# Image attention: the last 32 keys of four sub-steps gathered, turned by one transpose and weighed by values padded with zeros

## The chip, the cores and the metric

One Trainium2 chip, one core of it. The metric is the device time of one execution in microseconds (us). All times below are of that core.

## What is computed

The reference is a chain of eight gated layers on an image sequence `x` (4 batches, 512 tokens, width 128), each with its own attention or feed-forward part. The change touches the first one alone:

```python
def _layernorm(x, axis=-1, eps=1e-05): ...
def _L0_xattn_ref(image_embeds, latents, ln1_g, ln1_b, ln2_g, ln2_b, Wq, Wkv, Wo):
    x = layer_norm(image_embeds, ln1_g, ln1_b)      # context: 4 x 154 x 128
    l = layer_norm(latents, ln2_g, ln2_b)           # latents: 4 x 512 x 128
    q = l @ Wq
    kv_in = jnp.concatenate([x, l], axis=1)         # 666 keys
    k, v = jnp.split(kv_in @ Wkv, 2, axis=-1)
    # 16 heads of 64; softmax(q k / 8) v; heads joined; @ Wo
x = x + jnp.tanh(g_xattn[0]) * _L0_xattn_ref(ctx_1024, _layernorm(x, axis=-1), ...)
```

Every one of the 512 queries of a batch attends to 666 keys, the 512 latents and the 154 context rows, in 16 heads of width 64. 666 keys are five tiles of 128 and a rest of 26.

## The kernel before

All eight layers run one after the other as one program. Each engine has its own instruction stream, written out by hand; streams meet only in semaphores, and every engine does its instructions in the order of its stream.

**The unit of work in the first layer.** Two heads are projected together, a *group* (32 of them: 4 batches of 8 pairs). A group has two *units* of 256 queries (64 units), and a unit four *sub-steps*, (h, j) = (0,0), (0,1), (1,0), (1,1): one head h and one tile of 128 queries j each (256 sub-steps). The streams all loop over `image_steps()`, and the loop index i is the sub-step whose scores are made. In iteration i:

- TensorE (`image_pe`, L593) makes the scores of sub-step i (`image_scores_pe`, L683: four bf16 matmuls, into one of two slots of two PSUM banks). If i % 4 is 0 it weighs tiles 0 to 2 of the unit two back, if it is 2 tiles 3 to 5 (`image_weigh_pe`, L709), and then turns the two spread tiles (L615). Then it turns the probabilities of sub-step i-2 (`image_turn_pe`, L694): six fp32 transposes, four into bank 4, two into bank 5 (the last of 26 rows). In even iterations comes one of the four parts of the next group's projection (`image_project_pe`, L475, into bank 7).
- VectorE (`image_ve`, L715) multiplies the finished unit by its inverse sums (L740, if i % 4 is 3), takes the largest score of sub-step i from PSUM (L744), in odd iterations makes the low bf16 halves of the projection part (`image_lows_ve`, L798 to L813), takes the reciprocal of the sums (L752, if i % 4 is 0), and copies bank 5 of sub-step i-2 to SBUF (L758, the event `kept_b`). For sub-step (0,0) it also makes the low half of these two tiles itself (L763, `low_c`).
- ScalarE (`image_ac`, L816) makes the exponentials of sub-step i (L837; it waits for the maximum), keeps the spread tiles (L846, if i % 4 is 2; once per unit), copies bank 4 of sub-step i-2 to SBUF (L852, `kept_a`), and keeps the high halves of the projection part (`image_keep_ac`, L881 to L895).
- GpSimd (`image_po`, L897) spreads the inverses (L934), splits the finished unit (L942), and makes the low halves of the turned probabilities of sub-step i-3: tiles 0 to 3 (L963, 512 wide, `low_a`) and, except for (0,0), tiles 4 and 5 (L963, 256 wide, `low_b`). In the first 160 iterations or so it also splits the next layer's weights, one piece every fourth iteration (L979, L980, L983).

**Products are three bf16 matmuls** (high by low, low by high, high by high), so a tile of probabilities is weighed by 3 matmuls a head: 64 columns of values as the weights, 256 queries as the moving side. The two heads of the pair write the two halves of the partitions of bank 6. A unit has 6 x 3 x 2 = 36 of them.

**Banks.** Banks 4 and 5 are single: the transposes of a sub-step wait for `kept_a` and `kept_b` of the sub-step before (`low_c` in place of `kept_b` after (0,0)). Bank 7 is single too: a projection part waits until VectorE has made the lows of the part before.

Beside the regular iterations there are chores once per batch: the layer norms of the next batch on VectorE (L405 to L421) and its transposes, and the output projection of the batch before (eight pairs by three matmuls for each of four tiles, L475), which shares bank 7.

Of the kernel before, what the change touches and what calls it, by code (L numbers as in the profile page):

```python
# [9 lines left out]
ALU = mybir.AluOpType  # L10
# [126 lines left out]
def constants():  # L137
# [33 lines left out]
    for part in range(3):  # L171
# [18 lines left out]
        "clear": "filled", "tokens": "filled", "wo_low": "filled", "mixed_low": "low_b", "summed": "router_steps", "ranked": "routed",  # L190
        "places": "placed", "clean": "router_steps", "padded": "router_steps", "relative": "router_steps", "delta": "router_steps",
# [33 lines left out]
class Kernel:  # L225
# [293 lines left out]
    def image_memory(self):  # L519
# [3 lines left out]
        self.v = [self.place(KT0, 2, P, dt=BF16) for _ in range(3)]  # L523
# [3 lines left out]
        self.probs_t = [self.place(2, KT0, 2 * P) for _ in range(2)]  # L527
        self.sums = [self.place(4) for _ in range(4)]
        self.inverse = [self.place(4) for _ in range(2)]
# [3 lines left out]
        self.probs_parts = [t.rearrange("p h t n -> p (h t n)").bitcast(BF16).rearrange("p (h t n s) -> p h t n s", h=2, t=KT0, s=2)  # L533
# [59 lines left out]
    def image_pe(self, pe):  # L593
        w = self.w[0]
        pe.wait_ge(*self.at("dma_const", 16))
        pe.wait_ge(*self.at("clean", 1))
# [9 lines left out]
        for i in self.image_steps():  # L606
# [3 lines left out]
            if back is not None:  # L610
                self.image_weigh_pe(pe, back, ((0, 1, 2), None, (3, 4, 5))[part])
# [29 lines left out]
    def image_project_pe(self, pe, n, part):  # L641
# [12 lines left out]
        elif part == 2:  # L654
            self.bank(pe, 7, "v_low", 3 * n + 2)
# [7 lines left out]
            m = self.products(pe, side[:, 3 * P:4 * P], lambda s: c[:, s, c0 + P:c0 + 2 * P], lambda s: values[s], True, True)  # L663
        else:
            self.bank(pe, 7, "v_low", 3 * n + 3)
# [20 lines left out]
    def image_turn_pe(self, pe, i):  # L686
        prob = self.probs[i % 3]
        pe.wait_ge(*self.at("exp", i + 1))
        for bank, tiles, name in ((4, range(0, 4), "kept_a"), (5, range(4, KT0), "kept_b")):
            ps = self.bank(pe, bank, *((name, i) if bank == 4 or (i % 4) else ("low_c", i // 4)))  # L690
            for t in tiles:
                rows = min(P, KEYS0 - t * P)
                c = (t - tiles[0]) * P
                m = pe.transpose(ps[0:rows, c:c + P], prob[:, t * P:t * P + rows], self.eye)  # L694
            m.then_inc(self.mark("turned_a" if bank == 4 else "turned_b"))

    def image_weigh_pe(self, pe, u, tiles):
        n = u // 2
        if tiles[0] == 0:
            pe.wait_ge(*self.at("low_a", 4 * u + 3))  # L700
            pe.wait_ge(*self.at("v_low", 3 * n + 3))
            self.bank(pe, 6, "mixed", u + 1)
        else:
            pe.wait_ge(*self.at("low_b", 4 * u + 3))
            pe.wait_ge(*self.at("low_c", u))
        for t in tiles:
            for which, (of_values, of_probs) in enumerate(((0, 1), (1, 1), (0, 0))):
                for h in (0, 1):
                    m = pe.matmul(self.out_bank[64 * h:64 * h + 64, 0:2 * P], self.v[n % 3][:, t, of_values, 64 * h:64 * h + 64],  # L709
                                  self.probs_parts[u % 2][:, h, t, :, of_probs], start=t == 0 and which == 0,  # L710
                                  stop=t == KT0 - 1 and which == 2)
        if tiles[-1] == KT0 - 1:
            m.then_inc(self.mark("weighed"))

    def image_ve(self, ve):  # L715
        x, xn = self.x, self.xn
        ve.memset(self.bank_b, 0.0).then_inc(self.mark("clean"))
        for v in self.v:
            ve.memset(v[:, KT0 - 1, :, :], 0.0)
# [15 lines left out]
        for i in self.image_steps():  # L735
# [12 lines left out]
            if back is not None and part == 0:  # L748
# [3 lines left out]
                ve.reciprocal(self.inverse[back % 2], self.sums[back % 4]).then_inc(self.mark("inverted"))  # L752
            if 2 <= i < SUBS + 2:
                u, _, _, _, h, j = self.image_sub(i - 2)
                if u >= 2:
                    ve.wait_ge(*self.at("weighed", u - 1))
                ve.wait_ge(*self.at("turned_b", i - 1))
                ve.tensor_copy(self.probs_t[u % 2][:, h, 4:KT0, j * P:(j + 1) * P],  # L758
                               self.bank_b[:, 0:2 * P].rearrange("p (t n) -> p t n", t=2)).then_inc(self.mark("kept_b", i - 2))
                if (h, j) == (0, 0):  # L760
# [136 lines left out]
    def image_po(self, po):  # L897
# [68 lines left out]
        for _ in pieces:  # L966
            pass
# [1832 lines left out]
```

## Time and profile before

| what | value |
|---|---|
| median of 3 runs | 1933.74 us (1933.63 to 1936.42) |
| profiled execution, its own time | 1927.72 us |
| its span, first to last instruction | 1925.9 us |
| mean granted TensorE clock | 0.875 |
| busy share of the span: TensorE, VectorE, ScalarE, GpSimd | 78%, 61%, 42%, 39% |
| the first layer's attention in the span | about 35 to 712 us |
| busiest groups | GpSimd L963 372.6 us, TensorE L694 218.0, VectorE L744 216.3, ScalarE L837 209.2 |

In the profile a duration is that of one instruction from start to end. Instructions of one engine overlap at their ends, so what an instruction costs in a busy stream is the distance from its start to the next start, which is shorter. "PEld" is TensorE's weight load. An idle time in brackets stands before the instruction, with what ended it; "issue" is time in which the engine waited for nothing that the profile shows.

### The profile page before, as it was taken

To read this page: it belongs to the slowest core of one execution; us is meant where nothing else is said; L and a number is where in the kernel's file an instruction comes from. 1 tells how busy PE (TensorE), PEld (TensorE's weight loads), DVE (VectorE), ACT (ScalarE), POOL (GpSimd) and SP (SyncE) were. 2 spreads that over 40 slices of the span, in tenths; PEclk is the share of its full clock that TensorE was granted. 3 is DMA by queue.
4 is the path that set the end of the run, shared out by engine and by line. 5 is a ranking of instruction groups with operands and counts; after the bars stand their busy time and mean duration, and the time that the engine had idled before them with its cause. 6 is when DMAs were issued, how large, how long until landed. Compare 5 with 4: busy or idle time off the path is not lost.

```text
span 1925.9 us, 31970 instructions
## 1 busy us (share of the span) xinstructions
PE 1497.9 (78%) x11459; PEld 982.9 (51%) x11581; DVE 1175.3 (61%) x2856; ACT 802.1 (42%) x1803; POOL 754.6 (39%) x906
## 2 busy tenths in 40 slices
PE   4899979979998977574278789958976885568877
PEld 2677757766776765452255345524443333324444
DVE  4777677767767655538847657644565555644443
ACT  3677657747765644320034245533212542201111
POOL 3688678857756863500012343000002101233330
PEclk9999999999999997776568799989986987778887
DMA  6233211211211112400000000000000000000000
GB/s 241 63 102 106 74 55 42 55 36 38 54 41 45 52 33 72 161 5 1 0 1 1 11 4 1 1 1 1 1 1 1 1 1 1 1 0 6 1 6 11
DMA packets 35442, 63.93 MB, mean 33 GB/s; under 512 B 7527, under 2 KB 25026, under 8 KB 34131
## 3 DMA queue, kind: packets, MB, share of 16 engines
q1 hardware_dynamic: 33815, 59.77, 10.4%
q0 software_dynamic: 1472, 2.12, 0.4%
q8 instruction: 95, 1.56, 0.3%
q14 instruction: 60, 0.49, 0.1%
HBM read 30.59 MB, written 12.66 MB: 22 GB/s over the span
## 4 chain that ended last, share of the span: by engine, by line
PE 63%; DVE 23%; issue 4%; POOL 4%; ACT 4%; DMA 1%; SPq 0%; DVEq 0%; ACTq 0%; POOLq 0%
PE banks L475 15%; PE banks L694 8%; PE banks L709 6%; PE banks L683 6%; PE banks L1876 3%; DVE xn L421 3%; PE banks L1859 2%; PE banks L450 2%; DVE work L744 2%; PE banks L2546 2%; DVE norm_room L405 1%; PE banks L2497 1%; PE banks L1785 1%; PE banks L1826 1%; POOL work L963 1%
## 5 line engine op out<-in xcount | busy, mean ns | idle before, releaser
L963 POOL TENSOR_TENSOR work<-work 128x512 bf16<-128x512 f32 (+1 forms) x448 | 372.6, 861 | 48.3 <-ACT work L852 45.0
L837 ACT ACTIVATE work<-banks,work 128x666 f32<-128x666 f32 x256 | 209.2, 817 | 200.6 <-DVE work L744 165.7
L415 POOL TENSOR_TENSOR norm_room<-norm_room,minus_half 128x4 f32<-128x4 f32 x48 | 50.1, 1044 | 542.3 <-DVE norm_room L410 542.3
L744 DVE TENSOR_REDUCE work<-banks 128x1 f32<-128x666 f32 x256 | 216.3, 845 | 61.2 <-PE banks L683 60.8
L694 PE MATMUL banks<-const,work 128*128 128x128 f32 (+1 forms) x1536 | 218.0, 279 | 31.2 <-ACT work L852 26.1
L694 PEld LDWEIGHTS banks<-const,work 128*128 128x128 f32 (+1 forms) x1536 | 155.9, 135 | 53.0 <-ACT work L837 29.4
L758 DVE COPY work<-banks 128x256 f32<-128x256 f32 x256 | 106.9, 418 | 122.2 <-PE banks L694 122.1
L683 PE MATMUL banks<-work 128*128 128x154 bf16 (+1 forms) x932 | 170.6, 302 | 11.5 <-DMA work<-work 6.4
L475 PE MATMUL banks<-work,weights_b 128*128 128x512 bf16 (+1 forms) x830 | 157.4, 347 | 13.3 <-DVE work L2200 5.6
L709 PE MATMUL banks<-work 128*64 128x256 bf16 x2304 | 158.6, 282 | 8.3 <-POOL work L963 7.1
L852 ACT ACTIVATE work<-banks 128x512 f32<-128x512 f32 x256 | 151.2, 591 | 9.5 <-PE banks L694 9.4
L450 PE MATMUL banks<-const,xn 128*128 128x128 f32 x176 | 40.7, 374 | 141.4 <-DVE xn L421 89.3
L683 PEld LDWEIGHTS banks<-work 128*128 128x128 bf16 x1024 | 98.1, 99 | 88.6 <-DMA work<-work 6.6
L1953 DVE TENSOR_REDUCE work<-banks 128x2 f32<-128x308 f32 x192 | 86.8, 473 | 79.2 <-PE banks L1831 45.1
L709 PEld LDWEIGHTS banks<-work 128*64 128x64 bf16 x2304 | 120.4, 110 | 28.1 <-POOL work L963 10.2
L456 ACT ACTIVATE xt<-banks 128x512 f32<-128x512 f32 x48 | 28.7, 597 | 246.3 <-PE banks L450 246.1
L475 PEld LDWEIGHTS banks<-work,weights_b 128*128 128x128 bf16 (+1 forms) x840 | 83.0, 100 | 83.9 <-issue 18.3
L2688 POOL TENSOR_TENSOR work<-work 128x512 bf16<-128x512 f32 x64 | 66.3, 1043 | 142.8 <-DVE work L2645 142.8
L1932 ACT ACTIVATE work<-banks 128x256 f32<-128x256 f32 (+1 forms) x256 | 87.4, 382 | 59.5 <-PE banks L1863 26.9
L450 PEld LDWEIGHTS banks<-const,xn 128*128 128x128 f32 x176 | 26.7, 187 | 153.6 <-DVE xn L421 72.6
L1859 PE MATMUL banks<-work 128*128 128x256 bf16 (+1 forms) x256 | 66.4, 292 | 14.1 <-ACT work L1924 11.6
L475 PE MATMUL banks<-weights_c 128*128 128x128 bf16 (+2 forms) x288 | 65.9, 260 | 0.0
(390 smaller groups left out, 3006.8 us busy)
## 6 DMA issues: line engine op xcount, KB each, us to landing
work<-work SPq DMA_DIRECT2D x128, 166.5 KB, 3.0
sorted<-in_pads SPq DMA_DIRECT2D x10, 838.5 KB
weights_b<-in_weights SPq DMA_DIRECT2D x1, 4120.0 KB, 23.9
work<-scratch SPq DMA_DIRECT2D x64, 64.0 KB, 2.0
weights_b<-in_weights SPq DMA_DIRECT2D x1, 2824.0 KB, 9.8
weights_a<-in_weights SPq DMA_DIRECT2D x1, 2056.0 KB, 8.5
weights_a<-in_weights SPq DMA_DIRECT2D x1, 2050.0 KB, 10.1
work<-work SPq DMA_DIRECT2D x32, 64.0 KB, 1.9
```

Of the source, the lines that this page charges most:

```text
L450: i = pe.transpose(ps[:, j * P:j * P + rows], src[0:rows, j, :], self.eye[0:rows, 0:rows])
L475: m = pe.matmul(out, left(a), right(b), start=start and n == 0, stop=stop and n == 2)
L683: m = pe.matmul(slot[:, a:z], lhs, k[:, h, part, a:z], start=part == 0, stop=part == 1)
L694: m = pe.transpose(ps[0:rows, c:c + P], prob[:, t * P:t * P + rows], self.eye)
L709: m = pe.matmul(self.out_bank[64 * h:64 * h + 64, 0:2 * P], self.v[n % 3][:, t, of_values, 64 * h:64 * h + 64], self.probs_parts[u % 2][:, ...
L744: ve.tensor_reduce(self.neg_max[i % 4], self.slot[i % 2][:, 0:KEYS0], AX_X, ALU.max, negate=True).then_inc(self.mark("max"))
L758: ve.tensor_copy(self.probs_t[u % 2][:, h, 4:KT0, j * P:(j + 1) * P], self.bank_b[:, 0:2 * P].rearrange("p (t n) -> p t n", t=2)).then_inc ...
L837: ac.activation(self.probs[i % 3], self.slot[i % 2][:, 0:KEYS0], ACT.Exp, bias=self.neg_max[i % 4], accum_out=self.sums[u % 4][:, 2 * j + ...
L852: ac.activation(self.probs_t[u % 2][:, h, 0:4, j * P:(j + 1) * P], self.bank_a.rearrange("p (t n) -> p t n", t=4), ACT.Copy).then_inc(self ...
L963: po.tensor_tensor(parts[:, :, :, 0], exact, parts[:, :, :, 1], ALU.subtract).then_inc(self.mark(event, i - 3))
L1859: m = pe.matmul(bank, left, a.q4[b % 2][:, g, cols], start=True, stop=s != 4)
L1932: ac.activation(out, self.bank_of(k, HALF)[0:rows_n, :], ACT.Exp).then_inc(self.mark("exp4", s, n))
```

## The change

Keys 634 to 665, the last 32 of the 666, are taken out of the tiles. After its exponentials each sub-step has these 32 columns copied by VectorE into a quarter of a 128-wide tile `rest` in SBUF. After the fourth sub-step of a unit this tile is turned by one transpose, kept, and split once. It then holds four quarters of 32 rows, one for each (h, j). The weighing of tile 5 is replaced by six matmuls of 128 columns by 128 queries: for each j a value tile of 128 rows that holds the 32 keys of head 0 in quarter j, columns 0 to 63, those of head 1 in quarter 2 + j, columns 64 to 127, and zeros elsewhere. The full tiles are five, and in the fifth the values of its last 6 keys are zero, since the rest holds them. The four-fold last context rows are made by GpSimd once per batch (`four_times_po`), so that one projection yields the values in all four quarters; these are then kept by ScalarE and subtracted by VectorE in four pieces of 32 x 64 in place of one of 26 x 128.

The sixth transpose of each sub-step falls away, VectorE's copy of bank 5 is 128 wide in place of 256, its `low_c` moves from sub-step (0,0) to (1,1), where it is a 128-wide copy and a 128-wide subtraction, and GpSimd makes tile 4 of all four sub-steps, 128 wide. The clearing of bank 5 at the start, and TensorE's wait for it, are gone.

```diff
@@ -520,17 +520,19 @@
...
-        self.v = [self.place(KT0, 2, P, dt=BF16) for _ in range(3)]
+        self.v = [self.place(KT0 + 1, 2, P, dt=BF16) for _ in range(3)]
...
-        self.probs_t = [self.place(2, KT0, 2 * P) for _ in range(2)]
+        self.probs_t = [self.place(2, KT0 - 1, 2 * P) for _ in range(2)]
+        self.rest, self.rest_t = ([self.place(P) for _ in range(2)] for _ in range(2))
...
+        self.ctx_last = self.place(2, P, dt=BF16)
...
-        self.probs_parts = [t.rearrange("p h t n -> p (h t n)").bitcast(BF16).rearrange("p (h t n s) -> p h t n s", h=2, t=KT0, s=2)
+        self.probs_parts = [t.rearrange("p h t n -> p (h t n)").bitcast(BF16).rearrange("p (h t n s) -> p h t n s", h=2, t=KT0 - 1, s=2)
@@ -608,7 +609,7 @@
...
-                self.image_weigh_pe(pe, back, ((0, 1, 2), None, (3, 4, 5))[part])
+                self.image_weigh_pe(pe, back, ((0, 1, 2), None, (3, 4))[part])
@@ -652,7 +653,7 @@
...
-            self.bank(pe, 7, "v_low", 3 * n + 2)
+            self.bank(pe, 7, "v_low", 6 * n + 5)
@@ -660,9 +661,11 @@
...
-            m = self.products(pe, side[:, 3 * P:4 * P], lambda s: c[:, s, c0 + P:c0 + 2 * P], lambda s: values[s], True, True)
+            if n % PAIRS == 0:
+                pe.wait_ge(*self.at("four_times", b))
+            m = self.products(pe, side[:, 3 * P:4 * P], lambda s: self.ctx_last[:, s, :], lambda s: values[s], True, True)
...
-            self.bank(pe, 7, "v_low", 3 * n + 3)
+            self.bank(pe, 7, "v_low", 6 * n + 6)
@@ -686,37 +689,44 @@
...
-        for bank, tiles, name in ((4, range(0, 4), "kept_a"), (5, range(4, KT0), "kept_b")):
-            ps = self.bank(pe, bank, *((name, i) if bank == 4 or (i % 4) else ("low_c", i // 4)))
-            for t in tiles:
-                rows = min(P, KEYS0 - t * P)
-                c = (t - tiles[0]) * P
-                m = pe.transpose(ps[0:rows, c:c + P], prob[:, t * P:t * P + rows], self.eye)
-            m.then_inc(self.mark("turned_a" if bank == 4 else "turned_b"))
+        ps = self.bank(pe, 4, "kept_a", i)
+        for t in range(4):
+            m = pe.transpose(ps[:, t * P:(t + 1) * P], prob[:, t * P:(t + 1) * P], self.eye)
+        m.then_inc(self.mark("turned_a"))
+        ps = self.bank(pe, 5, *(("kept_b", i) if i % 4 < 3 else ("low_c", i // 4)))
+        m = pe.transpose(ps[:, 0:P], prob[:, 4 * P:5 * P], self.eye)
+        if i % 4 == 3:
+            pe.wait_ge(*self.at("gathered", i))
+            m = pe.transpose(ps[:, P:2 * P], self.rest[i // 4 % 2], self.eye)
+        m.then_inc(self.mark("turned_b"))
...
-            pe.wait_ge(*self.at("v_low", 3 * n + 3))
+            pe.wait_ge(*self.at("v_low", 6 * n + 6))
...
+        orders = ((0, 1), (1, 1), (0, 0))
...
-            for which, (of_values, of_probs) in enumerate(((0, 1), (1, 1), (0, 0))):
+            for which, (of_values, of_probs) in enumerate(orders):
...
-                    m = pe.matmul(self.out_bank[64 * h:64 * h + 64, 0:2 * P], self.v[n % 3][:, t, of_values, 64 * h:64 * h + 64],
-                                  self.probs_parts[u % 2][:, h, t, :, of_probs], start=t == 0 and which == 0,
-                                  stop=t == KT0 - 1 and which == 2)
-        if tiles[-1] == KT0 - 1:
+                    pe.matmul(self.out_bank[64 * h:64 * h + 64, 0:2 * P], self.v[n % 3][:, t, of_values, 64 * h:64 * h + 64],
+                              self.probs_parts[u % 2][:, h, t, :, of_probs], start=t == 0 and which == 0, stop=False, skip_group_check=True)
+        if tiles[-1] == KT0 - 2:
+            rest = self.halves(self.rest_t[u % 2])
+            for of_values, of_probs in orders:
+                for j in (0, 1):
+                    m = pe.matmul(self.out_bank[:, j * P:(j + 1) * P], self.v[n % 3][:, KT0 - 1 + j, of_values, :], rest[:, :, of_probs],
+                                  start=False, stop=(of_values, of_probs) == orders[-1], skip_group_check=True)
...
-        ve.memset(self.bank_b, 0.0).then_inc(self.mark("clean"))
...
-            ve.memset(v[:, KT0 - 1, :, :], 0.0)
+            ve.memset(v[:, KT0 - 2:, :, :], 0.0)
@@ -750,17 +760,22 @@
...
+            if 1 <= i < SUBS + 1:
+                u, s = (i - 1) // 4, (i - 1) % 4
+                if s == 0 and u >= 2:
+                    ve.wait_ge(*self.at("turned_b", 4 * u - 4))
+                ve.wait_ge(*self.at("exp", i))
+                ve.tensor_copy(self.rest[u % 2][:, 32 * s:32 * (s + 1)], self.probs[(i - 1) % 3][:, KEYS0 - 32:]).then_inc(self.mark("gathered", i - 1))
...
-                ve.tensor_copy(self.probs_t[u % 2][:, h, 4:KT0, j * P:(j + 1) * P],
-                               self.bank_b[:, 0:2 * P].rearrange("p (t n) -> p t n", t=2)).then_inc(self.mark("kept_b", i - 2))
-                if (h, j) == (0, 0):
-                    ve.wait_ge(*self.at("kept_b", i - 2))
-                    parts = self.probs_parts[u % 2][:, h, 4:KT0, 0:P, :]
-                    ve.tensor_tensor(parts[:, :, :, 0], self.bank_b[:, 0:2 * P].rearrange("p (t n) -> p t n", t=2), parts[:, :, :, 1],
+                ve.tensor_copy(self.probs_t[u % 2][:, h, 4, j * P:(j + 1) * P], self.bank_b[:, 0:P]).then_inc(self.mark("kept_b", i - 2))
+                if (h, j) == (1, 1):
+                    whole = self.rest_t[u % 2]
+                    ve.wait_ge(*self.own("ve", ve.tensor_copy(whole, self.bank_b[:, P:2 * P])))
+                    ve.tensor_tensor(self.halves(whole)[:, :, 0], self.bank_b[:, P:2 * P], self.halves(whole)[:, :, 1],
@@ -790,11 +805,19 @@
...
+    def value_pieces(self):
+        out = [(KT0 - 2, slice(0, CTX - 32), slice(0, P), slice(2 * P, 3 * P))]
+        for h, j in ((0, 0), (0, 1), (1, 0), (1, 1)):
+            r, c = 32 * (2 * h + j), 64 * h
+            out.append((KT0 - 1 + j, slice(r, r + 32), slice(c, c + 64), slice(3 * P + c, 3 * P + c + 64)))
+        return out
...
-            ve.wait_ge(*self.at("v_kept", 3 * n + 3))
+            ve.wait_ge(*self.at("v_kept", 6 * n + 6))
@@ -806,12 +829,11 @@
...
-            ve.wait_ge(*(self.at("k_high", 2 * n + 1) if part == 1 else self.at("v_kept", 3 * n + 2)))
+            ve.wait_ge(*(self.at("k_high", 2 * n + 1) if part == 1 else self.at("v_kept", 6 * n + 5)))
...
-            ve.tensor_tensor(v[:, 4, 1, :], side[:, 2 * P:3 * P], v[:, 4, 0, :], ALU.subtract).then_inc(self.mark("v_low"))
-            ve.tensor_tensor(v[0:CTX_REST, 5, 1, :], side[0:CTX_REST, 3 * P:4 * P], v[0:CTX_REST, 5, 0, :],
-                             ALU.subtract).then_inc(self.mark("v_low"))
+            for tile, rows, cols, src in self.value_pieces():
+                ve.tensor_tensor(v[rows, tile, 1, cols], side[rows, src], v[rows, tile, 0, cols], ALU.subtract).then_inc(self.mark("v_low"))
@@ -889,8 +911,8 @@
...
-                ac.activation(v[:, 4, 0, :], side[:, 2 * P:3 * P], ACT.Copy).then_inc(self.mark("v_kept"))
-                ac.activation(v[0:CTX_REST, 5, 0, :], side[0:CTX_REST, 3 * P:4 * P], ACT.Copy).then_inc(self.mark("v_kept"))
+                for tile, rows, cols, src in self.value_pieces():
+                    ac.activation(v[rows, tile, 0, cols], side[rows, src], ACT.Copy).then_inc(self.mark("v_kept"))
@@ -915,6 +937,8 @@
...
+                po.wait_ge(*self.at("ctxn_low", 1))
+                self.four_times_po(po, 0)
@@ -940,6 +964,8 @@
...
+            if (i + 10) % (8 * PAIRS) == 0 and (i + 10) // (8 * PAIRS) < BATCH:
+                self.four_times_po(po, (i + 10) // (8 * PAIRS))
@@ -953,10 +979,8 @@
...
-                for tiles, event in (((0, 4), "low_a"), ((4, KT0), "low_b")):
+                for tiles, event in (((0, 4), "low_a"), ((4, KT0 - 1), "low_b")):
...
-                        if (h, j) == (0, 0):
-                            continue
@@ -965,6 +989,15 @@
...
+    def four_times_po(self, po, b):
+        if b:
+            po.wait_ge(*self.at("projected", 4 * (PAIRS * b - 1) + 3))
+        for s in (0, 1):
+            i = po.tensor_copy(self.ctx_last[:, s, :].rearrange("p (r k) -> p r k", r=4),
+                               self.ctxn_parts[:, s, (b + 1) * CTX - 32:(b + 1) * CTX].unsqueeze(1).to_broadcast([P, 4, 32]))
+        i.then_inc(self.mark("four_times", b))
...
```

## Rows read from the trace of the kernel before

**Rows 1.** Busy time by window: us, busy (x count) of PE, PEld, DVE, ACT, POOL; PEclk, DMA, GB/s.

```profile
300.00:355.00 55.00, 53.63 (x541) 41.13 (x548) 40.10 (x85) 41.11 (x96) 48.09 (x64) 1.00 0.20 50
```

**Rows 2.** Timeline of ScalarE: the once-per-unit L846, first and last of ten.

```profile
464.41 0.38 ACT L846 ACTIVATE work<-banks 128x256 f32<-128x256 f32 x1
...
546.67 0.37 ACT L846 ACTIVATE work<-banks 128x256 f32<-128x256 f32 x1
```

**Rows 3.** Timeline of all engines, 308 to 317 us: start, us, engine, line, operation.

```profile
308.22 0.85 DVE L744 TENSOR_REDUCE work<-banks 128x1 f32<-128x666 f32 x1 [0.72 <-PE banks L683]
...
308.99 0.68 DVE L806 SCALAR_TENSOR_TENSOR scratch<-banks,work 128x512 bf16<-128x512 f32 x1
...
309.59 0.41 DVE L758 COPY work<-banks 128x256 f32<-128x256 f32 x1
...
309.92 0.84 DVE L744 TENSOR_REDUCE work<-banks 128x1 f32<-128x666 f32 x1
...
310.86 0.82 ACT L837 ACTIVATE work<-banks,work 128x666 f32<-128x666 f32 x1 [0.29 <-DVE work L744]
...
311.66 0.38 ACT L846 ACTIVATE work<-banks 128x256 f32<-128x256 f32 x1
311.68 0.42 DVE L758 COPY work<-banks 128x256 f32<-128x256 f32 x1 [0.92 <-PE banks L694]
...
311.93 0.60 ACT L852 ACTIVATE work<-banks 128x512 f32<-128x512 f32 x1
...
312.13 0.45 DVE L763 TENSOR_TENSOR work<-banks,work 128x256 bf16<-128x256 f32 x1
...
312.48 0.41 DVE L740 TENSOR_TENSOR work<-banks,work 128x256 f32<-128x256 f32 x1
312.64 0.59 PEld L694 LDWEIGHTS banks<-const,work 128*128 128x128 f32 x6
...
312.82 0.85 DVE L744 TENSOR_REDUCE work<-banks 128x1 f32<-128x666 f32 x1
...
314.01 0.94 PEld L709 LDWEIGHTS banks<-work 128*64 128x64 bf16 x18
...
314.57 0.59 ACT L852 ACTIVATE work<-banks 128x512 f32<-128x512 f32 x1
315.27 0.59 PEld L694 LDWEIGHTS banks<-const,work 128*128 128x128 f32 x6 [0.33 <-issue]
...
317.30 0.85 DVE L744 TENSOR_REDUCE work<-banks 128x1 f32<-128x666 f32 x1 [0.61 <-PE banks L683]
```

**Rows 4.** The same timeline one unit on, 321.72 us: the second transposes of that unit.

```profile
321.72 0.59 PEld L694 LDWEIGHTS banks<-const,work 128*128 128x128 f32 x6
```

**Rows 5.** The chain that ended last, pieces in the first layer: start, us, what.

```profile
47.73 0.20 DVE work L812
47.93 0.18 DVE work L813
...
217.35 1.40 PE banks L475 x24
...
308.18 0.66 PE banks L694 x6
...
309.40 1.14 PE banks L709 x18
```

**Rows 6.** Groups by line and shape, 200 to 360 us: GpSimd's two forms of L963.

```profile
L963 POOL TENSOR_TENSOR work<-work 128x512 bf16<-128x512 f32 x60 | 62.6, 1043 | 4.7 <-ACT work L852 4.1
...
L963 POOL TENSOR_TENSOR work<-work 128x256 bf16<-128x256 f32 x45 | 27.8, 618 | 0.0
```

**Rows 7.** Line L421 (fp32, SBUF to SBUF): ns min/median/max; then one beside GpSimd's L980.

```profile
L421 DVE TENSOR_SCALAR xn<-x,work x16: 344/651/1080, 6.3 to 429.5; 128x128 f32<-128x128 f32 x16
...
242.60 1.32 DVE L421 TENSOR_SCALAR xn<-x,norm_room 128x128 f32<-128x128 f32 x1
...
242.68 1.16 POOL L980 TENSOR_TENSOR split<-weights_b,split 128x512 bf16<-128x512 f32 x1
```

More of the change, by code:

```diff
@@ L189 @@
         "bq_scaled": "filled", "bv_wide": "filled", "clear_shift": "filled", "context_rest": "filled", "ones": "filled",
-        "clear": "filled", "tokens": "filled", "wo_low": "filled", "mixed_low": "low_b", "summed": "router_steps", "ranked": "routed",
-        "places": "placed", "clean": "router_steps", "padded": "router_steps", "relative": "router_steps", "delta": "router_steps",
+        "clear": "filled", "tokens": "filled", "four_times": "filled", "wo_low": "filled", "mixed_low": "low_b", "summed": "router_steps", "ranked": "routed",
+        "places": "placed", "gathered": "placed", "padded": "router_steps", "relative": "router_steps", "delta": "router_steps",
         "mix": "router_steps", "gates": "gate_steps", "gate_exp": "gate_steps"}
@@ L595, in image_pe @@
         pe.wait_ge(*self.at("dma_const", 16))
-        pe.wait_ge(*self.at("clean", 1))
         self.turn(pe, ("in", 0), self.xn[:, 0:QT, :], 0, ("in", 0, 1))
```

## The prediction, made before the changed kernel ran

> **What bounds the kernel now.** I read the busy time by window first: in a quiet stretch of the first layer TensorE is busy 53.63 of 55 us, GpSimd 48.09 (87%), VectorE and ScalarE about 40 [rows 1]. That looks like a kernel that TensorE bounds, and every us taken off TensorE would be a us gained. So I looked at what releases TensorE inside a unit. A unit takes (546.67 - 464.41) / 9 = 9.14 us [rows 2]; 39 of the 64 units lie within 9.1 to 9.4, about 13 longer ones are set by the chores on VectorE, 12 are others (first, last, and those with the output projection).
>
> In the timeline [rows 3] two places tell. ScalarE's kept_a starts at 311.93 and lasts 0.60, so ends at 312.53; TensorE's next transposes load at 312.64. The next kept_a ends at 314.57 + 0.59 = 315.16 and the next transposes load at 315.27. Both times 0.11 behind the release, a semaphore's way. At the second place the weighing began at 314.01 and its 18 matmuls take 1.14 [rows 5], so TensorE was free at 315.15 and stood for 0.12: ScalarE, not TensorE, set that start. So TensorE's full load and two loops through the other engines are nearly equal in length, and the question is what the change does to each loop.
>
> Loop 1, the one that closes now: transposes of (0,0) done, kept_b 311.68 (VectorE idled 0.92 for it), low_c 312.13, the unit's product 312.48, maximum 312.82, exponentials, kept_a 314.57, transposes 315.27, then TensorE's own work to the next (0,0).
>
> Loop 2: maximum at 308.22, projection lows 308.99, kept_b 309.59, maximum 309.92, exponentials 310.86, spread kept 311.66, kept_a 311.93, transposes 312.64, then TensorE's scores, weighing, transposes, projection and scores to the maximum at 317.30. Its only slack is the 0.12 before 315.27. One unit later the transposes load at 321.72 [rows 4], 4.42 behind the maximum at 317.30; here 312.64 - 308.22 = 4.42 too. The loop's VectorE and ScalarE half is the same stiff 4.42 in both units.
>
> **TensorE's part.** A transpose costs 0.66 / 6 = 0.11 [rows 5]. Three of 24 a unit fall away: -0.33. Of the weighing 6 matmuls of 1.14 / 18 = 0.063 go, 0.38, and 6 of 128 x 128 come, which in a projection cost 1.40 / 24 = 0.058 [rows 5], 0.35: -0.03. Together -0.36 a unit, 23 us over 64 units if TensorE alone counted. Switching the array from 64 to 128 columns is done now too, behind the weighing. Loop 2 holds only the transposes of (0,1) and (1,0), so it gets -0.22. Loop 1 gets -0.25 from TensorE, and on VectorE kept_b shrinks and low_c leaves its path: 0.80 from kept_b to product becomes 0.20, so -0.85 in all.
>
> **VectorE's part in loop 2**, between the maximum at 308.22 and that at 309.92. Start to start a 128-wide subtraction from PSUM costs 0.20, a 26-row one 0.18 [rows 5], the 256-wide kept_b 309.92 - 309.59 = 0.33 [rows 3]: 1 ns an element over a base of 0.07.
> - kept_b at half the width: 0.33 to 0.20, -0.13.
> - low_c now stands right behind it, in iteration (0,1), ahead of the next maximum: a copy whose end is waited for, 0.42 - 0.13 + 0.03 (312.13 is 0.03 past the end of a copy of 0.42) = 0.32, and a subtraction of 0.20: +0.52.
> - the gather, 32 wide from SBUF: 0.10 unhindered, +0.10.
> - every second unit the value lows: four of 32 x 64 at 0.135 in place of one of 0.18, +0.36, or +0.18 a unit.
>
> Sum +0.67 a unit, against -0.22 from TensorE and 0.12 of slack: loop 2 grows by 0.33. The other three gathers sit where VectorE idles for TensorE (0.92, 0.72 and 0.61 in these rows).
>
> **The gather's wait for GpSimd.** No row shows a 32-wide SBUF copy while GpSimd works. The nearest is L421, also one fp32 source in SBUF and an SBUF destination: 0.34 at the least, median 0.65, and the one at 242.60 took 1.32, ending 0.08 past GpSimd's L980 that ran from 242.68 to 243.84 [rows 7]. It stands until the GpSimd instruction is over. The subtractions from PSUM and the maximum keep one duration throughout. At the gather in loop 2 GpSimd is inside its run of L963, pieces of 1.04 [rows 6] and of about 0.40 after the change (0.618 less half the step from 256 to 512, 0.21). Bounds: 0 if so short a copy is not held, 1.04 if it always just misses. I take the mean rest of a piece met at random, (1.04² + 0.40²) / (2 x 1.44) = 0.43, since form and place are L421's.
>
> The Trainium skill, SBUF — State Buffer, section "Who interferes with whom", says why: an fp32 copy inside SBUF uses a port pair that GpSimd shares, and the second to come is blocked for a whole instruction. By that rule each gather waits, the sum is the forecast's; without it the sum is the first rival's. It speaks against just this step, and L421 agrees. The same skill, Perfetto Trace Analysis, section "Optimizing Scalar/DVE Operations", gives VectorE about 0.125 us overhead an instruction on PSUM, more than my base of 0.07; by it the pieces and the extra copy would cost about 0.2 a unit more. The sum goes by the rows.
>
> **The rest.** GpSimd: three L963 of 0.618 become four of 0.40, -0.25 a unit, on an engine that idles 13%; no gain. The four-fold rows are two copies a batch, eight in all, each below the 0.62 of a wider operation, at worst 5 us, taken at 0: TensorE asks for them two projection parts later at the start, ten iterations later afterwards. ScalarE gets three more small activations every second unit, right ahead of exponentials for which it now idles on VectorE: 0, at worst 0.16 x 1.5 x 39 = 9 us (0.16 estimated as 0.20 less the half width). The clearing of bank 5 and the wait for it lie ahead of the first data: 0. TensorE's wait for the gathered tile: the copy is made an iteration earlier, 0.
>
> **Sum.** 39 quiet units x (0.33 + 0.43) = +30. 13 units set by VectorE: its own sum (gathers +0.40, kept_b -0.52, low_c +0.17, pieces +0.18) is +0.2, and about one of the four gathers a unit waits on the path, +0.43: +0.6, +8. 12 others, where TensorE or loop 1 counts: -0.36, -4. In all about +33 us on the profiled execution's 1927.72, which lies 6 us under the median; set on the median of 1933.74: about 1966 us.
>
> **Rivals.**
> - *The same loop, but the gather is not held up.* Loop 2 grows by 0.33 only: 13 + 3 - 4 = +12, 1945 us. For it: a copy of 32 elements may slip between two GpSimd pieces, and VectorE's reciprocals never grow. Against: L421. Chance 0.26.
> - *TensorE stays the bound and the work saved is gained.* That asks that the additions in loop 2 come to less than 0.22 + 0.12 = 0.34 a unit, half my 0.67. Then 51 units give 0.36: -18 us, 1915 us. For it: TensorE's 53.63 of 55. Against: 0.11 behind kept_a each time, and low_c's 0.52 alone is over the point. Chance 0.14. It would be the other sign.
> - *Both even out*, additions near 0.34 with no wait: within 0.2% (3.9 us, about what a measurement of this kernel can tell from no change), 1934 us. Chance 0.08.
>
> **How the numbers follow.** The forecast has 0.52: its own range runs from 1950 to 1990 (the wait between 0.1 and 1.04 a unit). With the port-free rival and the even case the range reaches down to 1930; what lies below it is the faster case, 0.14, and some 0.04 lies above 1990. Slower is 0.52 + 0.26 = 0.78, same 0.08, faster 0.14.
>
> **What would show it.** Right: a quiet unit takes 9.5 to 10.2 between two L846; TensorE idles for ScalarE ahead of the transposes of (0,1), near half a us and more; gathers of 0.2 and of up to 1 us stand side by side, the long ones ending with a GpSimd instruction; from one maximum to the next in iteration (0,1) 2.2 us or more in place of 1.70. Wrong: a unit below 9.1 us with kept_a early (TensorE did bind), gathers all near 0.2 (no shared port), or VectorE's copy and subtraction hidden in idle time.

## The result and the profile after

The changed kernel takes **1984.88 us** (median of 4 runs, 1977.53 to 1989.29) against 1933.68 for the kernel before in the same session: ratio **1.025, 95% interval 1.0223 to 1.0277**. The forecast of 1966 us (ratio 1.017) had the sign and the mechanism, and was 19 us short. The profiled run took 1977.53 us, the shortest of the four, with a span of 1975.7. TensorE's busy time over the whole span is as before (1496.8 us, 1497.9 before), in a longer span. The page of the changed kernel:

```profile
PE 1496.8 (76%) x11267; PEld 968.6 (49%) x11389; DVE 1230.3 (62%) x3271; ACT 822.1 (42%) x1899; POOL 741.0 (38%) x978
...
PE 53%; DVE 30%; issue 6%; ACT 6%; POOL 3%; DMA 1%; ACTq 0%; DVEq 0%; SPq 0%; POOLq 0%
...
L859 ACT ACTIVATE work<-banks,work 128x666 f32<-128x666 f32 x256 | 209.2, 817 | 227.2 <-DVE work L754 187.8
...
L694 PE MATMUL banks<-const,work 128*128 128x128 f32 x1024 | 163.8, 284 | 74.3 <-ACT work L874 74.1
L694 PEld LDWEIGHTS banks<-const,work 128*128 128x128 f32 x1024 | 111.2, 143 | 102.1 <-ACT work L859 75.8
```

The second line is the share of each engine in the chain that ended last; TensorE had 63% and VectorE 23% before. In the groups, TensorE now idles 74.3 us ahead of its transposes (31.2 before), nearly all for ScalarE's kept_a, and ScalarE idles 227.2 us ahead of the exponentials, 187.8 of them for VectorE's maximum (200.6 and 165.7 before). VectorE is busy 1230.3 us where it was 1175.3, ScalarE 822.1 where it was 802.1: VectorE got more to do, and the other two wait for it. The window that answers to [rows 1], same columns:

```profile
300.00:355.00 55.00, 47.83 (x468) 34.94 (x475) 40.99 (x112) 37.34 (x89) 42.24 (x62) 1.00 0.19 48
```

TensorE fell from 53.63 to 47.83 of 55 us at the same granted clock. To see the size, units are measured as in [rows 2], start to start of ScalarE's once-per-unit instruction, now L868:

```profile
334.89 0.38 ACT L868 ACTIVATE work<-banks 128x256 f32<-128x256 f32 x1
345.29 0.38 ACT L868 ACTIVATE work<-banks 128x256 f32<-128x256 f32 x1
355.38 0.37 ACT L868 ACTIVATE work<-banks 128x256 f32<-128x256 f32 x1
...
536.96 0.38 ACT L868 ACTIVATE work<-banks 128x256 f32<-128x256 f32 x1
547.21 0.37 ACT L868 ACTIVATE work<-banks 128x256 f32<-128x256 f32 x1
556.52 0.38 ACT L868 ACTIVATE work<-banks 128x256 f32<-128x256 f32 x1
```

The units alternate. One of each pair has VectorE's 512-wide projection lows in its loop, call it P; the other has the value lows, call it V. And there are two stretches: the *early* one, from about 120 to 480 us, in which GpSimd also splits the next layer's weights (L1012, L1013, L1016), and the *late* one. All in us a unit:

| | before | after | forecast |
|---|---|---|---|
| P, early / late | 9.21 / 9.21 | 10.09 / 9.31 | +0.15 and a wait of 0.43 |
| V, early / late | 9.08 / 9.08 | 10.40 / 10.16 | +0.51 and a wait of 0.43 |

(The forecast's 0.33 is 0.15 without value pieces and 0.51 with them.) The first three quiet units, ahead of the weight splits, take 9.30, 10.16 and 9.32, as the late ones do. By one profile of each kernel the 26 quiet units up to 480 us (20 of them in the early stretch) cost +25.0 us, the 11 behind them +8.7, the 26 other units +15.1, and 2.4 came ahead of the first: 51.2 us.

The timeline of an early P unit, with GpSimd, in the place of [rows 3]:

```profile
330.30 0.85 DVE L754 TENSOR_REDUCE work<-banks 128x1 f32<-128x666 f32 x1 [0.85 <-PE banks L686]
...
331.06 0.68 DVE L829 SCALAR_TENSOR_TENSOR scratch<-banks,work 128x512 bf16<-128x512 f32 x1
...
331.32 1.16 POOL L1013 TENSOR_TENSOR split<-weights_b,split 128x512 bf16<-128x512 f32 x1
...
331.66 0.85 DVE L768 COPY work<-work 128x32 f32<-128x32 f32 x1
...
332.43 0.28 DVE L774 COPY work<-banks 128x128 f32<-128x128 f32 x1
...
332.63 0.27 DVE L777 COPY work<-banks 128x128 f32<-128x128 f32 x1
...
332.94 0.31 DVE L778 TENSOR_TENSOR work<-banks,work 128x128 bf16<-128x128 f32 x1
333.15 0.84 DVE L754 TENSOR_REDUCE work<-banks 128x1 f32<-128x666 f32 x1
...
334.09 0.82 ACT L859 ACTIVATE work<-banks,work 128x666 f32<-128x666 f32 x1 [1.45 <-DVE work L754]
...
335.87 0.20 PEld L694 LDWEIGHTS banks<-const,work 128*128 128x128 f32 x2 [1.22 <-ACT work L859]
```

This is loop 2 as forecast. From maximum to maximum it takes 333.15 - 330.30 = 2.85 where [rows 3] had 1.70; ScalarE's exponentials stand 1.45 for it, and TensorE's transposes 1.22 for ScalarE (the view names L859, but kept_a, L874, ends at 335.76, 0.11 ahead of them, as in the prediction). The gather (L768, 32 columns) lasts 0.85: it ends at 332.51, with GpSimd's weight split L1013 that runs from 331.32 to 332.48. In the early V units the gather lasts about 0.42 and ends with a GpSimd L987 (342.38 + 0.41, beside 341.71 + 1.05). The late stretch shows the loop without that hold. VectorE alone, first a V unit, then a P unit:

```profile
522.78 0.85 DVE L754 TENSOR_REDUCE work<-banks 128x1 f32<-128x666 f32 x1 [0.75 <-PE banks L686]
523.55 0.31 DVE L833 TENSOR_TENSOR work<-banks,work 128x154 bf16<-128x154 f32 x1
523.78 1.17 DVE L836 TENSOR_TENSOR work<-banks,work 122x128 bf16<-122x128 f32 x5
524.97 0.18 DVE L768 COPY work<-work 128x32 f32<-128x32 f32 x1
525.18 0.29 DVE L774 COPY work<-banks 128x128 f32<-128x128 f32 x1
...
525.91 0.84 DVE L754 TENSOR_REDUCE work<-banks 128x1 f32<-128x666 f32 x1
...
552.60 0.85 DVE L754 TENSOR_REDUCE work<-banks 128x1 f32<-128x666 f32 x1 [0.85 <-PE banks L686]
553.37 0.68 DVE L829 SCALAR_TENSOR_TENSOR scratch<-banks,work 128x512 bf16<-128x512 f32 x1
553.97 0.17 DVE L768 COPY work<-work 128x32 f32<-128x32 f32 x1
554.05 0.28 DVE L774 COPY work<-banks 128x128 f32<-128x128 f32 x1
554.25 0.28 DVE L777 COPY work<-banks 128x128 f32<-128x128 f32 x1
554.57 0.30 DVE L778 TENSOR_TENSOR work<-banks,work 128x128 bf16<-128x128 f32 x1
554.78 0.84 DVE L754 TENSOR_REDUCE work<-banks 128x1 f32<-128x666 f32 x1
```

P: 2.18 from maximum to maximum; the forecast's terms give 1.70 - 0.13 + 0.52 + 0.10 = 2.19. V: 3.13, where the kernel before has 1.72 and the terms give 1.72 + 0.49 + 0.36 = 2.57. Here 0.56 is missing, and it lies between 523.78 and 525.18. The five value lows take 1.19 up to the gather, where the forecast's prices (0.20 and four times 0.135) give 0.74, and the gather costs 0.21 up to the next start, where it costs 0.08 in the P unit. (The V unit at 542.26, whose 3.21 the expectations below quote, is the exception of the late stretch: its gather lasts 0.26 and ends with a GpSimd copy, L998.) So two things were open: how much the hold by GpSimd is worth in all, and why four small subtractions cost what they do.

### The profile page after: what moved, and what is told of

Its sections match the earlier page's. It is cut to its first block, busy times and chain, and to the rows that moved or that the text cites. A ratio compares the mean times of both kernels' runs of the same rounds, so it can differ in the third digit from the quotient of the medians.

```text
span 1975.7 us, 32231 instructions
## 1 busy us (share of the span) xinstructions
PE 1496.8 (76%) x11267; PEld 968.6 (49%) x11389; DVE 1230.3 (62%) x3271; ACT 822.1 (42%) x1899; POOL 741.0 (38%) x978
## 4 chain that ended last, share of the span: by engine, by line
PE 53%; DVE 30%; issue 6%; ACT 6%; POOL 3%; DMA 1%; ACTq 0%; DVEq 0%; SPq 0%; POOLq 0%
PE banks L475 13%; PE banks L694 4%; DVE work L754 4%; PE banks L716 4%; PE banks L686 4%; PE banks L1909 3%; DVE xn L421 3%; PE banks L450 2%; PE banks L1892 2%; DVE work L836 1%; PE banks L2579 1%; DVE work L768 1%; PE banks L1818 1%; PE banks L2530 1%; PE banks L1859 1%
## 5 line engine op out<-in xcount | busy, mean ns | idle before, releaser
L987 POOL TENSOR_TENSOR work<-work 128x512 bf16<-128x512 f32 (+1 forms) x512 | 356.7, 726 | 120.4 <-ACT work L874 118.3
L859 ACT ACTIVATE work<-banks,work 128x666 f32<-128x666 f32 x256 | 209.2, 817 | 227.2 <-DVE work L754 187.8
L694 PE MATMUL banks<-const,work 128*128 128x128 f32 x1024 | 163.8, 284 | 74.3 <-ACT work L874 74.1
L686 PE MATMUL banks<-work 128*128 128x512 bf16 (+1 forms) x938 | 177.4, 306 | 7.1 <-DMA work<-work 1.9
L694 PEld LDWEIGHTS banks<-const,work 128*128 128x128 f32 x1024 | 111.2, 143 | 102.1 <-ACT work L859 75.8
L874 ACT ACTIVATE work<-banks 128x512 f32<-128x512 f32 x256 | 151.2, 591 | 7.2 <-PE banks L694 7.2
L716 PE MATMUL banks<-work 128*64 128x256 bf16 x1920 | 138.2, 285 | 3.5 <-POOL work L987 2.4
L716 PEld LDWEIGHTS banks<-work 128*64 128x64 bf16 x1920 | 99.6, 111 | 23.6 <-POOL work L987 4.2
L774 DVE COPY work<-banks 128x128 f32<-128x128 f32 x256 | 72.6, 284 | 59.6 <-PE banks L697 57.2
L768 DVE COPY work<-work 128x32 f32<-128x32 f32 x256 | 83.7, 327 | 1.3 <-ACT work L859 0.3
L697 PE MATMUL banks<-const,work 128*128 128x128 f32 x256 | 73.5, 287 | 13.1 <-DVE work L778 13.0
```

Source lines behind the costliest of these rows:

```text
L686: m = pe.matmul(slot[:, a:z], lhs, k[:, h, part, a:z], start=part == 0, stop=part == 1)
L694: m = pe.transpose(ps[:, t * P:(t + 1) * P], prob[:, t * P:(t + 1) * P], self.eye)
L768: ve.tensor_copy(self.rest[u % 2][:, 32 * s:32 * (s + 1)], self.probs[(i - 1) % 3][:, KEYS0 - 32:]).then_inc(self.mark("gathered", i - 1))
L859: ac.activation(self.probs[i % 3], self.slot[i % 2][:, 0:KEYS0], ACT.Exp, bias=self.neg_max[i % 4], accum_out=self.sums[u % 4][:, 2 * j + ...
L874: ac.activation(self.probs_t[u % 2][:, h, 0:4, j * P:(j + 1) * P], self.bank_a.rearrange("p (t n) -> p t n", t=4), ACT.Copy).then_inc(self ...
L987: po.tensor_tensor(parts[:, :, :, 0], exact, parts[:, :, :, 1], ALU.subtract).then_inc(self.mark(event, i - 3))
```

## The experiments

In each, the ratio is to the kernel before, run in the same session (its median went from 1933.7 to 1941.2 between sessions); one thousandth is 1.94 us.

### The hold by GpSimd

**e1_reduce**: the gather as a reduction over one element.

```diff
- ve.tensor_copy(rest[...], probs[..., KEYS0 - 32:])
+ ve.tensor_reduce(rest[...], probs[..., KEYS0 - 32:].unsqueeze(2), AX_X, ALU.max)
```

> The changed kernel, with the gather of 32 columns written as a maximum over one element instead of a copy; same place, same data. If the copy waits for GpSimd at the port that both use, the reduction does not: every gather then takes about 0.15 to 0.2 us, quiet units in the first half fall from 10.09 and 10.40 to the 9.3 and 10.15 that the second half already shows, and the kernel takes 1985 - 26 x 0.4 - about 5 in the units with chores = 1967 to 1972 us. If the long gathers are only the price of one more instruction, nothing changes: 1985 us.

1968.38 us, ratio 1.0135 (1.0106 to 1.0163): 0.0115, 22 us, below the changed kernel. The group of L768 in the changed kernel (ns min/median/max), and then in this one:

```profile
L768 DVE COPY work<-work x256: 141/193/3528, 40.1 to 753.9; 128x32 f32<-128x32 f32 x128
```

```profile
L768 DVE TENSOR_REDUCE work<-work x256: 150/176/188, 40.9 to 737.4; 128x32 f32<-128x32 f32 x128
```

The copy takes up to 3.53 us, the reduction of the same 32 columns never over 0.19. Units are now 9.32 (P) and 10.17 (V) in both stretches: the early stretch lost 0.77 and 0.23, the late one nothing (one late unit of 10.66 apart). So GpSimd's hold is real, is the whole difference between the stretches, and costs a mean of 0.50 a quiet early unit, 10 us for the 20 of them. In the two profiles the layer's attention is 16.5 us shorter; the 22 of the ratios is uncertain by about 8.

The longest copy of the changed kernel outlasts any single GpSimd instruction. It ends at 691.75, when a gapless run of five of them (687.96 to 691.70) is over:

```profile
687.96 3.74 POOL L987 TENSOR_TENSOR work<-work 128x512 bf16<-128x512 f32 x5
688.22 3.53 DVE L768 COPY work<-work 128x32 f32<-128x32 f32 x1
```

### The value pieces

**e11_pieces_128** and **e12_pieces_same_rows** change only the rows that VectorE's four small value pieces cover (two runs each). Both leave the values' low halves in some rows other than the computation asks.

```diff
  for tile, rows, cols, src in self.value_pieces():
+     rows = rows if tile < KT0 - 1 else slice(0, P)     # e11
+     rows = rows if tile < KT0 - 1 else slice(0, 32)    # e12
      ve.tensor_tensor(v[rows, tile, 1, cols], side[rows, src], v[rows, tile, 0, cols], ALU.subtract)
```

> The changed kernel with VectorE's four small value pieces taken 128 partitions high and 64 columns wide in place of 32 by 64, so that they no longer start on different partitions. They also fill the rows that should stay zero in the low halves, so the values' low part is not the reference's there. If it is the change of partition rows that makes an instruction wait for the end of the one before, the pieces stand about 0.14 apart in place of 0.25, the maximum-to-maximum time of an iteration with pieces falls from 3.21 to about 2.75, and the time by 10 to 15 us. If a small instruction simply costs 0.25, nothing changes.

1972.32 us, ratio 1.0172 (1.0132 to 1.0213). Late V units take 9.64 in place of 10.16, early ones 10.27 in place of 10.40. The early ones gain little because their gather starts earlier but still ends with the same GpSimd instruction: it now lasts 0.88 in place of 0.42.

> The changed kernel with VectorE's four small value pieces all on partitions 0 to 31 (32 by 64 each, their columns and tiles as they were); the low halves of the other rows are left out. e11_pieces_128 took them 128 partitions high and brought their spacing from 0.25 down (five of L837 in 0.81 us in place of 1.16) and the maximum-to-maximum time of such an iteration from 3.21 to 2.60. It changed two things, the height and the starting partition. If the starting partition of neighbours counts, the pieces overlap here too: about 0.14 apart, 2.6 from maximum to maximum, 9.64 a unit with pieces, about 1972 us. If a 32-row instruction never overlaps, all stays at 0.25, 3.21, 10.16 and about 1985 us.

1971.48 us, ratio 1.0174 (1.0121 to 1.0227), units as in e11. VectorE in e12, to be laid beside the V unit above:

```profile
533.18 0.85 DVE L754 TENSOR_REDUCE work<-banks 128x1 f32<-128x666 f32 x1 [0.75 <-PE banks L686]
533.95 0.31 DVE L833 TENSOR_TENSOR work<-banks,work 128x154 bf16<-128x154 f32 x1
534.18 0.79 DVE L837 TENSOR_TENSOR work<-banks,work 122x128 bf16<-122x128 f32 x5
534.90 0.24 DVE L768 COPY work<-work 128x32 f32<-128x32 f32 x1
535.06 0.27 DVE L774 COPY work<-banks 128x128 f32<-128x128 f32 x1
...
535.77 0.84 DVE L754 TENSOR_REDUCE work<-banks 128x1 f32<-128x666 f32 x1
```

The five value lows take 0.72 up to the gather in place of 1.19, the forecast's 0.74. The gather behind them costs 0.16 here, ending with a GpSimd instruction at 535.11, and 0.08 in the V units where none is beside it. The maxima stand 2.59 apart (e11: 2.60), near the forecast's 2.57. The pieces are as small and as many as before; only the partitions they start on are now the same. So it is the change of rows from one instruction to the next that takes the overlap away, worth 0.0076, 15 us.

**e6_only_values**: the four 32 x 64 pieces are gone. ScalarE and VectorE keep and subtract one 128 x 128 tile, and four DMAs a group place its quarters. The first piece (122 x 128) stays; the cut is shortened.

```diff
- for tile, rows, cols, src in self.value_pieces(): ve.tensor_tensor(...)
+ ve.tensor_tensor(v_full[:, 1, :], side[:, 3 * P:4 * P], v_full[:, 0, :], ALU.subtract)
+ for tile, rows, cols, _ in self.value_pieces()[1:]: sp.dma_start(v[rows, tile, :, cols], v_full[rows, :, cols])
```

> The changed kernel with only the four value pieces replaced by one tile and four DMAs. Loop theory: the units that hold the pieces (every second one) lose four times 0.25 less 0.20 on VectorE, so 0.8 to 1.0 us each; 32 of them give 25 to 30 us, 1.011 to 1.013 of the kernel before. By the price I forecast for the pieces (0.135 each) it would be 0.34 a unit and 11 us.

1958.02 us, ratio 1.0094 (1.0069 to 1.0118): 0.0156, 30 us, off the changed kernel. V units fall to 9.27 early and 9.28 late; P units stay at 10.08 and 9.32. In the 37 quiet units this is (25.0 + 8.7) - (10.9 + 3.2) = 20 us, 0.53 a unit, three times the +0.18 that the sum gave the pieces. Beside what e12 takes off, this also takes off the pieces' number on VectorE and on ScalarE, and in the early units what the gather waited there; these aren't told apart.

### The place of low_c

**e3_before_low_c**: the kernel before, with `low_c` for (1,1) in place of (0,0) and GpSimd leaving out (1,1). No work is added.

```diff
-                 if (h, j) == (0, 0):
+                 if (h, j) == (1, 1):
```

> The kernel before, with nothing but the 256-wide subtraction low_c moved from sub-step (0,0) to (1,1) (GpSimd makes the other three). No work is added. If the loop from maximum to maximum is as tight as the trace says (0.12 us of slack), 0.35 + 0.12 us more in it cost 0.3 to 0.35 us a quiet unit: 39 x 0.33 = 13 us, 1943 to 1948 us. If TensorE bounds the kernel before, the move costs nothing: 1934 us.

1958.49 us, ratio 1.0088 (1.0054 to 1.0122): +17 us for moving one subtraction. Units go from 9.21 and 9.08 to 9.51 and 9.42. VectorE there:

```profile
337.03 0.85 DVE L744 TENSOR_REDUCE work<-banks 128x1 f32<-128x666 f32 x1 [0.72 <-PE banks L683]
...
338.40 0.41 DVE L758 COPY work<-banks 128x256 f32<-128x256 f32 x1
...
338.85 0.45 DVE L763 TENSOR_TENSOR work<-banks,work 128x256 bf16<-128x256 f32 x1
...
339.19 0.84 DVE L744 TENSOR_REDUCE work<-banks 128x1 f32<-128x666 f32 x1
```

2.16 from maximum to maximum in place of 1.70: +0.46 on VectorE, +0.30 and +0.34 on the unit. The difference is the slack of loop 2, 0.12 to 0.16, read as 0.12 in the prediction. This is the mechanism by itself.

**e2_low_c_later**: the changed kernel; the rest is turned with the next unit's (0,0), so that its copy and subtraction lie on loop 1 again.

> The changed kernel, with the gathered tile turned together with sub-step (0,0) of the next unit, so that its copy and subtraction stand in the iteration where VectorE waits for ScalarE anyway. If the loop from maximum to maximum bounds the unit, 0.52 us leave it and each quiet unit gives back up to that: 37 x 0.5 = 18 us, so about 1967 us. If what costs is VectorE's work wherever it stands, or TensorE's wait for the gathered tile, it stays at 1985 us.

1969.56 us, ratio 1.0141 (1.0109 to 1.0173): 0.0109, 21 us. P units 9.55 early and 8.79 late, V units 9.87 and 9.95. Early units of both kinds and late P units give back the whole 0.52, late V units only 0.21; why these give less was not followed up.

### All three, and what bounds then

**e4_all** joins e1 and e2 and makes the gathers in pairs, in even iterations where VectorE idles for the transposes. **e5_values_by_dma** is e4 with the values of e6.

```diff
- if 1 <= i < SUBS + 1:
+ for g in ((i - 2, i - 1) if i % 2 == 0 and 2 <= i < SUBS + 1 else ()):
```

> The changed kernel with three repairs: the gather as a reduction, two gathers together in even iterations where VectorE idles, and the gathered tile turned with the next unit's (0,0). Left in the loop are the narrower copy of bank 5 (-0.13) and, every second unit, the four value pieces (about +0.8). Loop theory: units with pieces near 9.4 us, the others near 8.8, mean 9.1, as before: 1930 to 1940 us. If VectorE's load as such or TensorE counts in another way than by the loop: above 1960 us.

> The kernel with the three repairs, and the four value pieces gone from VectorE and ScalarE: each keeps one 128 x 128 tile, and four small DMAs bring its pieces to the zero-padded tiles. Loop theory: the last addition to the loop from maximum to maximum is gone, so both kinds of unit fall to what TensorE needs, about 8.7 us against 9.14 before; 37 quiet units give 14 to 16 us, the kernel takes 0.99 of the kernel before. If the pieces cost nothing but their own place on VectorE, it stays at the kernel before (1.000).

e4: 1942.0 us, ratio 1.0005 (0.9981 to 1.0029), level with before. e5: **1925.66 us, ratio 0.9925 (0.9897 to 0.9952)**, faster than both kernels. But its units are 9.06 (P) and 8.97 (V), not the 8.7 hoped for. In e4 they are 8.71 and 9.77; e5 shortens the V units alone, and the P units get longer in answer, so a group falls from 18.48 to 18.03 and no further.

**e8_copy_in_idle**: e5 with plain copies as gathers.

> The kernel with all four repairs but the gather a plain copy again, two of them in even iterations. The copies will still be held by GpSimd, up to 1 us each. If place decides, VectorE's idle time there takes it up and the kernel stays within 5 us of the one with reductions; if the hold costs anywhere, 64 x 2 x 0.4 = 50 us more at the most.

1926.49 us, ratio 0.9922 (0.9895 to 0.9948), as e5. In VectorE's idle time the copy's hold costs nothing that shows; the place alone cures it.

**e7_transposes_back**: e5 with three transposes a unit made twice, 0.33 of TensorE's work.

> The kernel with all four repairs, with three transposes a unit done twice, so that TensorE has its old count again and nothing else changes. If this kernel is at last bound by TensorE, each unit gets 0.33 us back, 64 x 0.33 = 21 us at the most, 15 to 20 expected; if a loop still bounds it, less than 8.

1936.46 us, ratio 0.9961 (0.9939 to 0.9982): 7 us over e5 by the ratios, whose intervals overlap, and +0.11 a quiet unit in the profiles. That is a third of what TensorE alone would have made of it, and within the 8 us expected if a loop bounds. So e5 isn't bound by TensorE's work alone, nor quite free of it.

**e9_product_after_max** (e5) and **e10_before_product_after_max** (the kernel before) exchange the maximum and the unit's product, to take 0.41 off loop 1.

> The kernel of e5_values_by_dma, with one pair of VectorE's instructions exchanged: where the finished unit is multiplied by its inverse sums (once per unit), the maximum now goes first and the product behind it. In e5's timeline the product takes 0.41 from 527.75 to the maximum at 528.16, and the weighing that needs its bank begins only at 529.17. Theory 'loop 1 (transposes of (0,0), kept_b, the rest's copy and subtraction, product, maximum, exponentials, kept_a) bounds e5': a quiet unit goes from 9.02 to 8.7 or less and the time falls by 51 x 0.3 = about 15 us against e5, ratio to the kernel before near 0.985. Rival 'it is TensorE's own work with gaps of issue that bounds e5': the unit stays at 9.0 and the time within 3 us of e5's.

> The kernel before with the same exchange of product and maximum alone. Loop 1 loses 0.41 there, loop 2 has 0.12 of slack and TensorE is busy 8.9 of 9.14 a unit. If the forecast's picture of three nearly equal lengths holds, a unit goes from 9.14 to 9.02 and the time falls by about 5 us, ratio 0.997; more than 10 us would say that loop 2 had more slack than the 0.12 read ahead of its weighing, none at all that loop 1 was not the one that closed.

e9: 1927.18 us, ratio 0.9942 (0.9921 to 0.9964), no gain over e5 (units 9.19 and 9.00). e10: 1951.58 us, ratio 1.0061 (1.0043 to 1.008), a loss of 12 where 5 us of gain were forecast. The trace of e10 names a wait that I hadn't priced:

```profile
529.80 0.85 DVE L739 TENSOR_REDUCE work<-banks 128x1 f32<-128x666 f32 x1 [0.24 <-PE banks L683]
...
530.57 0.41 DVE L743 TENSOR_TENSOR work<-banks,work 128x256 f32<-128x256 f32 x1
...
531.10 0.98 PEld L709 LDWEIGHTS banks<-work 128*64 128x64 bf16 x18 [0.31 <-issue]
```

The product L743 ends at 530.98, and the weighing, which writes the bank that the product reads and waits for it by semaphore, begins at 531.10, 0.12 later: TensorE stands 0.31 in front of it, though the view calls it "issue". Ahead of the maximum the product had been done in time. And of the 0.41 taken off ahead of the maximum 0.24 comes back at once, as a wait for its scores. Loop 1 couldn't be shortened this way, so whether it alone bounds e5 stays open.

## Why the prediction was right, and where its sizes were off

- **What bounds.** Right. TensorE's 53.63 of 55 didn't mean that work taken off it is gained: it does less in a unit, idles for kept_a, and the unit is longer. e3 shows the near-equality of the loops with no work added.
- **TensorE's -0.36.** Its size wasn't measured alone; e7 says that such an amount moves the unit by a third of itself even in the best version.
- **VectorE's part in loop 2.** Right to 0.01 in the sum of a late P unit (2.18 against 2.19): kept_b 0.20, rest copy 0.32, subtraction 0.21, gather 0.08 where 0.10 was forecast.
- **The value pieces, 0.135 each, +0.18 a unit.** The step that failed most. The base of 0.07 with 1 ns an element was taken from instructions that start on the same partition, and these change partitions. On equal rows the five value lows keep to the forecast (0.72 against 0.74), on their own rows they take 1.19, and the gather behind them 0.13 more. V units took +1.07 late where +0.51 was forecast.
- **The overhead an instruction, by the Trainium skill.** Its page Perfetto Trace Analysis, section "Optimizing Scalar/DVE Operations", puts about 0.125 us of overhead on a VectorE instruction on PSUM; the prediction worked out 0.2 more a unit by it. The late units did take 0.585 a unit, the mean of 0.10 and 1.07, where the sum without a wait gave 0.33, so the rule's 0.2 comes near the total. But it gets there by another way: the P unit's rows needed no more than the base of 0.07, nor did the pieces on equal rows in e12, and all that was missing sat at the pieces on changing rows and right behind them.
- **The gather's wait for GpSimd, +0.43 on 39 units (17 us).** Right that there is such a wait, wrong in how it comes about and in its sum. The forecast let the gather meet GpSimd's L963 at a random point. In a periodic kernel nothing is random. The gather of late units passes L987 (the same line now) at its end or misses it and waits for nearly nothing. In early V units it meets one of them, 0.23 a unit, and the big wait, 0.77 in every early P unit, is for a weight split of 1.16 that the prediction did not count. That makes 10 us on the quiet units, and 22 over all by e1. The Trainium skill's rule in SBUF — State Buffer, section "Who interferes with whom", on which the prediction leaned, agrees in kind with the 3.53 against 0.19 of e1. The 3.53 spans five GpSimd instructions, though, where the prediction took one (1.04) as the most. The first rival, a gather that isn't held, falls for the early stretch and gives the right time for the late one, only because the gather meets so little there.
- **The others, +8 and -4.** Wrong in size: the 26 units with chores or output projection took +15.1, and the start +2.4. Of the 15.1, 5.5 go with the hold (e1: 9.6) and 6.6 with the pieces' rows (e12: 8.5), by the same measure from one profile each. The output projection's own unit does gain, 13.06 to 12.55, and the next gives it back, 14.17 to 15.48.
- **GpSimd's narrow piece, 0.40.** Measured 0.404 (x54). **ScalarE's pieces, 0**: in the late V unit above they end at 523.49, and ScalarE then still idles 0.24 for the maximum. The four-fold rows, 0: not separated from the rest.
- **The total.** Quiet units: +30 forecast, +33.7 measured. That these lie so near is luck: the wait was taken 7 us too high, and the pieces about 11 us too low (0.56 in each of 19 quiet V units). The chores, the output projection and the start, +17.5 where +4 was forecast, make most of the 19 us.

The other rivals, that TensorE stays the bound (1915 us) or that all evens out (1934), are excluded by the interval.

## What to carry to other kernels

Ahead of an edit that trades one engine's work for another's, measure the loops through all engines, not the busy shares: here 0.36 us a unit was taken from the busiest engine and 0.5 to 1.6 put on a loop with 0.12 of slack. A small helper instruction belongs where its engine idles anyway: the hold of the gathers cost about 22 us in the changed kernel and nothing that shows in the idle places of e8. Look up what stands *beside* the cost row: a base cost read from neighbours that start on the same partition doesn't hold for pieces that hop between partitions. And a wait in a periodic kernel is read from what stands beside it in each kind of unit; a mean over random meetings got it wrong both ways.

## What the runs showed of the hardware

- VectorE instructions of 32 x 64 on PSUM overlap when they start on the same partition (a 122 x 128 one and four of them take 0.72 us up to the next start, e12) and don't when each starts on another one (1.19 us, and 0.13 more on the gather behind them).
- A reduction over one element is a copy that GpSimd doesn't hold: 0.15 to 0.19 us in 256 cases, where the copy ran from 0.14 to 3.53. The 3.53 is as long as a run of five GpSimd instructions.
- Of 0.33 us of transposes added to a unit, 0.11 reached its length (e7): between nearly equal loops an addition is neither hidden nor paid in full.
